# Scan of a Mamba stage: decays from running sums that are fetched by DMA, the skip term on TensorE, and two PSUM banks for x

## The reference, cut to what matters

```
def _mamba2(u, Wi, conv_w, conv_b, dt_bias, A_log, D, norm_w, Wo):
    zxbcdt = u @ Wi.T
    z, xBC, dt = ...
    xBC = silu(conv(xBC, conv_w) + conv_b)        # 4 taps along time
    x = xBC[..., :256].reshape(b, L, 4, 64); Bm, Cm = ...   # 4 heads, state 128
    dt = softplus(dt + dt_bias)
    A = -exp(A_log)
    def step(h, inp):
        x_t, B_t, C_t, dt_t = inp
        dA = exp(dt_t * A)
        h = h * dA[..., None, None] + (dt_t[..., None] * x_t)[..., None] * B_t[:, None, None, :]
        y_t = einsum('bhpn,bn->bhp', h, C_t)
        return h, y_t
    ...
    y = y + D[None, None, :, None] * x            # the skip term
    y = y * silu(z)
    y = y * rsqrt(mean(y * y) + 1e-5) * norm_w
    return y @ Wo.T
```

## Time and profile before

| | |
|---|---|
| median of 3 runs | 875.42 us (875.26 to 875.46) |
| the profiled execution | 876.98 us, of which the span on the core is 875.2 us |
| TensorE, VectorE, ScalarE, GpSimd busy over the span | 740.4, 503.7, 551.9, 322.5 us |
| mean granted TensorE clock | 0.948 of 2.4 GHz |
| the scan | from about 486 to 709 us of the span |

### The profile page before, as it was taken

How to read it: one execution, slowest core, us unless ns; L and a number is a source line. 1 busy time by engine, 2 the same in 40 slices (tenths; PEclk the granted TensorE clock), 3 DMA queues, 4 the chain that set the end, 5 groups by cost and what they waited for, 6 DMA issues and landing times.

```text
span 875.2 us, 13632 instructions
## 1 busy us (share of the span) xinstructions
PE 740.4 (85%) x4304; PEld 393.6 (45%) x4304; DVE 503.7 (58%) x1483; ACT 551.9 (63%) x960; POOL 322.5 (37%) x352
## 2 busy tenths in 40 slices
PE   5799999989999879858889797998988958789981
PEld 1432222212232225535555464775766845456650
DVE  6876532115655748622657299786897957223341
ACT  5368987989989866422466776867867515234440
POOL 3090003301001424263123475664763831634343
PEclk9899999999999999988999998998999969889996
DMA  4057651621881211111210200000000011111313
GB/s 127 1 194 177 146 118 46 224 67 49 293 171 53 85 42 39 36 45 36 71 35 18 68 1 1 1 1 1 1 1 1 31 47 30 56 38 51 91 44 92
DMA packets 63372, 57.55 MB, mean 66 GB/s; under 512 B 8260, under 2 KB 51385, under 8 KB 63040
## 3 DMA queue, kind: packets, MB, share of 16 engines
q1 hardware_dynamic: 57888, 47.84, 19.7%
q0 software_dynamic: 5120, 8.68, 3.0%
q10 hardware_dynamic: 288, 0.10, 0.0%
HBM read 28.64 MB, written 29.05 MB: 66 GB/s over the span
## 4 chain that ended last, share of the span: by engine, by line
PE 29%; DVE 11%; issue 8%; POOL 6%; ACT 4%; DMA 2%; another core or an unknown queue 2%; SPq 0%; POOLq 0%; DVEq 0%; ACTq 0%
PE ps_main L1628 11%; PE ps_main L1658 7%; PE ps_side L1946 3%; DVE mb_act L1982 2%; PE ps_main L2014 1%; POOL moe_slots L1555 1%; PE ps_main L1589 1%; PE ps_main L1624 1%; DVE moe_hid L1653 1%; POOL mb_z L2158 1%; DMA moe_back<-moe_rows 1%; POOL mb_y_in L2156 1%; PE ps_main L1699 1%; POOL mb_h_dec L2100 1%
## 5 line engine op out<-in xcount | busy, mean ns | idle before, releaser
L685 ACT ACTIVATE attn_p<-attn_ps 128x1024 f32<-128x1024 f32 x256 | 240.6, 1057 | 35.3 <-PE attn_ps L701 22.7
L1628 PE MATMUL ps_main<-moe_xsT,moe_w 128*128 128x320 f32 x384 | 132.1, 473 | 24.9 <-DVE moe_hid L1653 18.3
L701 PE MATMUL attn_ps<-attn_p,attn_v 128*32 128x512 f32 x1024 | 137.4, 608 | 4.1 <-issue 3.9
L1653 DVE TENSOR_TENSOR moe_hid<-moe_act_h,ps_main 128x320 f32<-128x320 f32 (+1 forms) x128 | 62.0, 486 | 117.4 <-ACT moe_act_h L1638 56.2
L1638 ACT ACTIVATE moe_act_h<-ps_main 128x320 f32<-128x320 f32 (+1 forms) x128 | 55.0, 434 | 118.0 <-PE ps_main L1628 58.1
L1555 POOL DMA_INDIRECT moe_slots<-rows,moe_scatter_at x64 | 64.0, 1000 | 98.7 <-issue 30.7
L1628 PEld LDWEIGHTS ps_main<-moe_xsT,moe_w 128*128 128x128 f32 x384 | 71.2, 202 | 60.1 <-issue 40.7
L678 PE MATMUL attn_ps<-attn_q_rows,attn_k_rows 64*128 64x512 bf16 x448 | 84.5, 388 | 11.7 <-ACT attn_p L685 5.0
L678 PEld LDWEIGHTS attn_ps<-attn_q_rows,attn_k_rows 64*128 64x128 bf16 x448 | 20.3, 93 | 134.6 <-ACT attn_p L685 119.0
L1658 PE MATMUL ps_main<-moe_hid,moe_w 128*128 128x320 f32 (+1 forms) x256 | 75.2, 465 | 4.1 <-DVE moe_hid L1653 4.1
L1726 POOL DMA_INDIRECT moe_rows<-moe_y,moe_dest x48 | 46.2, 962 | 85.6 <-ACT moe_y L1719 63.0
(11 more groups left out here) (264 smaller groups left out, 1354.5 us busy)
## 6 DMA issues: line engine op xcount, KB each, us to landing
moe_slots<-zeros SPq DMA_DIRECT2D x4, 1380.0 KB, 12.6
attn_q_rows<-attn_q_parts SPq DMA_DIRECT2D x36, 128.0 KB
attn_k_rows<-attn_k_parts SPq DMA_DIRECT2D x36, 128.0 KB
moe_w<-in_w SPq DMA_DIRECT2D x3, 1536.0 KB, 11.3
moe_rows<-zeros SPq DMA_DIRECT2D x4, 1024.0 KB, 15.0
moe_back<-moe_rows SPq DMA_DIRECT2D x16, 256.0 KB, 3.3
...
```

The lines of the kernel that those rows point to most:

```text
L685: self.core.nc.scalar.activation(self.p[:, w % self.PB, :, :].rearrange("p a n -> p (a n)"), self.ps_s[:, w % self.SB, :, :].rearrange("p ...
L701: ins = self.core.nc.tensor.matmul(self.ps_av[32 * i:32 * i + 32, :], self.v[:, b * TPB + kt, HGROUPS * i + m, :], self.p[:, w % self.PB, ...
L1628: self.core.nc.tensor.matmul(ps[:, w % 2, 0:CAP], wt[:, e, c * P:(c + 1) * P], self.xsT[:, u % 2, :], start=True, stop=True).then_inc(self ...
L1653: self.core.nc.vector.tensor_tensor(self.hid[rows, u % 2, c, :], self.act_h[rows, w % 2, :], bank[rows, w % 2, 0:CAP], ALU.mult)\
```

## The change

`cut_a`, the matmuls of L2014 and L2027 and the Exp of L2044 go. Once for each sequence, TensorE makes the running sums of a's columns in two layouts (`sums`), ScalarE copies them and takes their Exp (`exp_sums`), and SP writes both to DRAM (`keep_rows`). For each chunk SP reads them back, broadcast over the partitions (`spread_rows`): 256 KB of sums, and 128 KB of their Exp in two transfers where i > 0. ScalarE makes the exponents by Relu(column − row) for each head, then Exp of the negative in place. The skip weights become two diagonal matrices a direction (`make_skips`), and TensorE adds the skip term into `ps_y`; the older part is added by VectorE in `back`, so `gate` has one operation. `ps_x` has two banks. The second sequence's step sizes come two chunks earlier. The semaphores of the setup stage are put together (not shown).

```diff
@@ sums (TensorE, once per sequence)
         for di in range(2):
-            nc.tensor.matmul(bank[:, di * n:(di + 1) * n], self.strict[:, di, :], self.a[:, tiles, di * NH:(di + 1) * NH], ...)
-        nc.tensor.matmul(bank[:, 2 * n:4 * n], self.ones[:], self.a[:, tiles, :], ...)
+            of = self.a[:, b, di, :, :].rearrange("p j h -> p (j h)")
+            nc.tensor.matmul(bank[:, di * n:(di + 1) * n], self.strict[:, di, :], of, ...)
+            nc.tensor.matmul(bank[:, (4 + di) * n:(5 + di) * n], self.incl[:, di, :], of, ...)
+            nc.tensor.matmul(bank[di * n:(di + 1) * n, 6 * n:6 * n + P], of, self.incl[:, di, :], ...)
+        nc.tensor.matmul(bank[:, 2 * n:4 * n], self.ones[:], self.a[:, b, :, :, :]...)
@@ exp_sums (ScalarE, once per sequence), after the three Exp that were there
+        nc.scalar.activation(self.cum[:, :, tiles, :], bank[:, 4 * n:6 * n]..., ACT.Copy).then_inc(self.decays, 1)
+        act.wait_ge(self.core.moe.combined, 2 * (b + 1))
+        if b:
+            act.wait_ge(self.rows_kept, 32 * b)
+        nc.scalar.activation(self.cum_rows[:, 0, :], rows, ACT.Copy).then_inc(self.decays, 1)
+        nc.scalar.activation(self.cum_rows[:, 1, :], rows, ACT.Exp).then_inc(self.decays, 1)
+    def keep_rows(self, sp, b):
+        sp.wait_ge(self.decays, self.DECAYS * (b + 1))
+        for k, into in enumerate((self.cum_dram, self.e_cum_dram)):
+            sp.dma_start(into[b]..., self.cum_rows[:, k, :]).then_inc(self.rows_kept, 16)
+        sp.wait_ge(self.rows_kept, 32 * (b + 1))
+    def spread_rows(self, sp, g):
+        if g >= 2:
+            sp.wait_ge(self.lowered, g - 1)
+        sp.dma_start(self.cums[:, g % 2, :, :], self.cum_dram[b, di, j]...to_broadcast([P, NH, P])).then_inc(self.cums_in[g % 2], 16)
+        if i == 0:
+            return
+        if g >= 2:
+            sp.wait_ge(self.y_read, g - 1)
+        for s in range(2):
+            sp.dma_start(self.e_cum[HP * s:HP * s + HP, g % 2, :, :], of_heads...to_broadcast([HP, 2, P])).then_inc(self.e_cum_in[g % 2], 16)
@@ step_sizes: a is written by two operations, one a direction
@@ before (TensorE)
-        pe.wait_ge(self.cut_done, NH * (g + 1))
-        if g >= 1:
-            pe.wait_ge(self.seg_exp, g)
-        for hh in range(NH):
-            ins = nc.tensor.matmul(self.ps_seg[...], self.cut[:, g % 2, hh, :], self.incl[:, di, :], ...)
         pe.wait_ge(self.act_ready, 4 * (u + 1))
-        if g >= 1:
-            pe.wait_ge(self.x_read, g)
-            pe.wait_ge(self.gm_done, g)
+        if g >= 2:
+            pe.wait_ge(self.x_read, g - 1)
+            pe.wait_ge(self.gm_done, g - 1)
         ...
-            pe.wait_ge(self.cb_read, g)
-        if i:
-            for hh in range(NH):
-                nc.tensor.matmul(self.ps_cb[...], self.a[...].to_broadcast([P, HP]), self.incl[:, di, :], ...)
+            pe.wait_ge(self.b_read, g)
@@ exps (ScalarE)
-        act.wait_ge(self.seg_done, g + 1)
+        act.wait_ge(self.cums_in[g % 2], 16 * (g // 2 + 1))
         if g >= 2:
             act.wait_ge(self.mt_done, g - 1)
-        nc.scalar.activation(self.e_seg[:, g % 2, :, :], self.ps_seg..., ACT.Exp).then_inc(self.seg_exp, 1)
-        act.wait_ge(self.cb_done, g + 1)
+        for hh in range(NH):
+            ins = nc.scalar.activation(self.e_seg[:, g % 2, hh, :], self.cums[:, g % 2, hh, :], ACT.Relu, bias=self.cum[:, di, n, hh:hh + 1], scale=-1.0)
+        ins.then_inc(self.lowered, 1)
+        act.wait_ge(self.b_done, g + 1)
-        if i:
-            nc.scalar.activation(self.e_cum[:, g % 2, :, :], self.ps_cb..., ACT.Exp)
         nc.scalar.copy(self.bs[:, g % 2, :], ...)
+        act.wait_ge(self.lowered, g + 1)
+        nc.scalar.activation(self.e_seg[:, g % 2, :, :], self.e_seg[:, g % 2, :, :], ACT.Exp, scale=-1.0).then_inc(self.seg_exp, 1)
@@ outputs (TensorE), after the wait for y_read
+        for c in range(2):
+            nc.tensor.matmul(self.ps_y[:, c * P:(c + 1) * P], self.skips[:, di, c * P:(c + 1) * P], self.act_t[:, u % 2, c, cols], start=(c == 0), stop=False)
@@ back (VectorE)
         if i:
-            (L2144) y_old = e_cum * ps_y
-        for c in range(2):
-            (L2146) y_in = act_t * skip + ps_y
+            dve.wait_ge(self.e_cum_in[g % 2], 32 * self.e_cums(g))
+            nc.vector.tensor_tensor(y_old, self.e_cum[:, g % 2, :, :], self.ps_y[:, 2 * P:4 * P]..., ALU.mult).then_inc(self.old_done, 1)
+            dve.wait_ge(self.old_done, self.carried(g))
+            nc.vector.tensor_tensor(y_in, y_old, own, ALU.add).then_inc(self.y_read, 1)
+        else:
+            nc.vector.tensor_copy(y_in, own).then_inc(self.y_read, 1)
@@ gate: the addition (L2156) and its wait are gone
@@ the streams
+  VectorE before the scan: make_skips, 4 operations of 128x128
-  ScalarE: cut_a(g) for g = 0, 1 before the last expert unit's weigh, cut_a(g + 2) in each chunk
-  TensorE u == 1: steps at i == 3, sums at i == 7
+  TensorE u == 1: steps at i == 1, sums at i == 3
-  VectorE u == 1: all four parts of step_sizes at i == 4
+  VectorE u == 1: part 0 at i == 1, parts 1 to 3 at i == 2
-  ScalarE u == 1: exp_dt at i == 4, exp_sums at i == 7
+  ScalarE u == 1: exp_dt at i == 2, exp_sums at i == 4
+  SP, after the load of the last expert unit: keep_rows(0), spread_rows(0), spread_rows(1),
+  the 1 MB fetch, then spread_rows(2) to (31) in order, with keep_rows(1) ahead of (16)
```

More of the change, by code:

```diff
@@ L1764 @@
     N = len(UNITS) * NC
+    DECAYS = 6
     PIECES = 6
@@ L1894, in weigh_out, with make_skips @@
                 ins = self.core.nc.vector.tensor_scalar(self.wo[:, di, c, :], self.wo[:, di, c, :], self.norm_w[:, di, c:c + 1], None, ALU.mult)
+        ins.then_inc(self.norm_done, 1)
+    def make_skips(self, dve):
+        core = self.core
+        core.landed(dve, "mb_skip", "ident")
+        dve.wait_ge(core.moe.y_done, B * E_ - 1)
+        for di in range(2):
+            for c in range(2):
+                ins = core.nc.vector.tensor_scalar(self.skips[:, di, c * P:(c + 1) * P], core.ident[:], self.skip[:, di, c:c + 1], None, ALU.mult)
         ins.then_inc(self.norm_done, 1)
@@ L2077, in to_state @@
         pool.wait_ge(self.x_read, g + 1)
-        pool.wait_ge(self.decays, 3 * (b + 1))
+        pool.wait_ge(self.decays, self.DECAYS * (b + 1))
         if self.carried(g) >= 2:
@@ L2401, in _ @@
                     if u == HALF - 1:
+                        mamba.keep_rows(sp, 0)
+                        for g in range(2):
+                            mamba.spread_rows(sp, g)
                         moe.fetch(sp, 1)
+                        for g in range(2, N):
+                            if g == 2 * NC:
+                                mamba.keep_rows(sp, 1)
+                            mamba.spread_rows(sp, g)
                 for half in range(2):
@@ L2499, in _ @@
                         mamba.weigh_out(dve)
-                dve.wait_ge(mamba.decays, 3)
+                mamba.make_skips(dve)
+                dve.wait_ge(mamba.decays, mamba.DECAYS)
                 dve.wait_ge(moe.y_turned, HALF)
@@ L2530, in _ @@
                         norm.normalise(dve, ch, i + 13)
-                    if u == 1 and i == 4:
-                        for part in range(mamba.STEP_PARTS):
+                    if u == 1 and i == 1:
+                        mamba.step_sizes(dve, ch, 1, 0)
+                    if u == 1 and i == 2:
+                        for part in range(1, mamba.STEP_PARTS):
                             mamba.step_sizes(dve, ch, 1, part)
@@ L2629, in _ @@
                 moe.keep(act, HALF - 1)
-                for g in range(2):
-                    mamba.cut_a(act, g)
                 moe.weigh(act, HALF - 1)
```

133 lines of the change are left out of this document (68 added, 65 removed).

## The result

The changed kernel takes 864.58 us (median of 5 runs, 858.66 to 866.22), the kernel before beside it 875.26 (873.03 to 875.46, 5 runs): a ratio of 0.9864, 95% interval 0.9829 to 0.9898. The forecast was 860.4, range 849 to 872, faster 0.87. By the medians the kernel is 10.7 us faster, where 15.0 were forecast.

A forecast was written before the change was run, and what follows sets the result against it. The prediction took VectorE to bound the middle of each unit, with gains mainly at starts and ends; terms of 16.3 us less 1.3 of costs gave 15.0, so 860.4 us from the median of 875.42, range 849 to 872.

The forecast's parts named there:

- TensorE's 1.14: Each of 28 chunks: TensorE loses 1.14 us net; in the 18 with convolutions VectorE covers it, so nothing moves.
- Start: Start of the scan: TensorE no longer waits for the bank of exponents; first convolution 2.5 us earlier, bounds 1 to 3.
- `back`: VectorE's step in each chunk: 0.85 us becomes 0.80, with copies saved in four chunks; 1.2 us together.
- (2): Chunk i = 2 of units 2 and 3: the 1.62 us wait for ScalarE's decays goes nearly whole; 3.1 for both.
- (3): Step sizes two chunks earlier: the same work of VectorE, 0.3 us of waiting less.
- (5): Ends of units 2 and 3: decays and SiLU come earlier; 1.4 and 2.5 us, together 3.9, bounds 1 to 6.
- (6): Starts of units 2 and 3, set by ScalarE up to the first tap: 0.7 and 1.9 us, together 2.6.
- (7): Head of unit 4: router work waits less for TensorE and VectorE's addition goes; 2.4 us, bounds 1 to 3.5.
- VectorE is relieved too: Rival: each of 18 chunks gets back up to 0.73 us in convolutions and L2069; 12 us more, 848; chance 0.15.
- 5.5 that the prediction allowed: Landing of the sums' transfer in each chunk: may take up to 5.5 us at no cost.
- The rival in which ScalarE's wait for the sums eats the ends: Unit ends give nothing because ScalarE waits for the sums instead of TensorE: 867 to 869 us, chance 0.17.
- below 0.9 in the middle: Sign of being wrong: TensorE's granted clock under 0.9 in the middle of a unit.

The follow-up runs named there:

- c3: The changed kernel with four dummy matmuls of L2014's shape added on TensorE in every chunk (about 1.0 us): 861.86 us, 0.9891 of the kernel before.
- a3: The changed kernel with the skip term back on VectorE and the addition back on GpSimd: 853.60 us, 0.999 of the kernel before.
- b1: The kernel before with only `make_skips`, the skip term on TensorE and the addition on VectorE: 854.21 us, 1.0015 of the kernel before.
- b3: The changed kernel with each transfer of the sums made twice in a row, SP waiting between: 867.65 us, 1.0167 of the kernel before.
- a2: The changed kernel with SP issuing the next chunk's sums ahead of this chunk's two decay transfers: 844.13 us, 0.9893 of the kernel before.
- a4: The changed kernel with the second sequence's step sizes in chunks i = 3 to 5 of unit 2, not 1 to 4: 850.0 us, 0.9949 of before.
- c2: The changed kernel with skip term on VectorE, addition on GpSimd, and ScalarE's square moved behind `take` and first tap: 871.62 us, 0.9966 of before.

## Why the prediction was right, and where it was not

- *VectorE bounds the middle; TensorE's 1.14 is hidden.* Right as far as the sign goes, and c3 shows it: 1.0 us put back in 32 chunks costs 2.8 us, not 20 or 32. Wrong in the picture: TensorE did not ride with slack, it stood level, 5.70 against 5.63. So the removed matmuls are worth almost nothing without the new body (a3: 1.5 us in the scan), and the skip term could be added only because they went (b1: a full chunk 0.5 longer).
- *The terms add up.* This is the step that failed. Exponents by DMA alone (with two banks and early step sizes) give 1.5 us of scan, the body alone 1.8, both 13.0. The sum of 15.0 treated its terms as each standing for itself. It came out near because it was asked for both parts at work only, and because its misses partly cancel; that much of the right number is luck.
- *The terms by stretch* (forecast before costs; measured in the two profiles). Start: 2.5; 1.6, the first convolution 1.85 earlier (19.0 us behind L1612 before, 17.1 after), inside the bounds 1 to 3. Unit 1: 0.6 (its end 0.3, `back`); 1.6. Unit 2: 4.3 ((2) 1.6, (3) 0.3, (5) 1.4, (6) 0.7, `back`); 1.8 and 3.0, since a wait of 1.77 (0.73 in the other profile) took the place of 1.62. Unit 3: 6.2 (1.5, 2.5, 1.9, `back`); 5.4 and 5.5. Unit 4: 2.6 ((7) and `back`); 2.6 and 1.4. So 16.3 less 1.3 against 13.0; the largest miss is unit 2, and the 1.77 the largest piece of it.
- *VectorE is relieved too* happened at a small size: in unit 1 L2113 takes 0.80 where it took 1.07 and a middle chunk 5.41 instead of 5.75, in all 1.6 us of that unit and not 0.7 a chunk. The mean of L2113 over the scan fell from 882 ns to 836, but with the addition back (a3) it is 815, so that mean says nothing about the addition. GpSimd's product took the place of the addition, as forecast: `gate` takes 0.72 us with no operation of VectorE beside it and 1.70 next to a convolution. The Trainium skill (SBUF — State Buffer, two separate sides) says that of an operation of GpSimd that reads SBUF and one of VectorE with two SBUF inputs the later one waits for the whole of the other. This trace agrees in that the two engines hold each other up (0.72 and 1.70); a whole hold for each addition removed did not come back.
- *The ends and the transfers.* The landing was taken as 2.6, it is 3.5 for 256 KB (2.6 for 64 KB); the issues 0.6 each, not 0.5. That is inside the 5.5 that the prediction allowed, and b3, at 7.4, loses about what the prediction set for it. The rival in which ScalarE's wait for the sums eats the ends has its wait (3.35 and 3.56 us), but a2 takes the wait away and gains nothing.
- *Step sizes earlier*, 0.3 gained: missed. The prediction counted only VectorE's work and left out that the step sizes' matmuls take a bank of `project`; VectorE waits 0.7 us for this, 1.8 at the low clock (a4). *Two banks*: 0 to 1 us, mostly at the start, where part of the 2.5 was.
- *Clock.* The mean of the scan fell from 0.94 to 0.90 (0.86 in a3, where TensorE waits most, 0.95 with the filler). In unit 1's stretch of convolutions it was 0.88, one of the signs that the prediction had named for being wrong (below 0.9 in the middle); yet VectorE covers it there. The lower share was forecast as a cost of 1.0. No run isolates the whole of it; the chunk compared under a4 alone shows 1.0 us, in one of two executions.

What stays open: how the 9 us of a3 beyond c2's 2.7 split between VectorE's own longer work, TensorE's wait for the paired squares and the clock; and where the medians lost 2.3 of the scan's 13.0.
